# Int8 weights prepared in the first attention, all its projections at the front, and a last stage that interleaves projection and feed-forward

## The chip, the core and the metric

The kernel runs on one core of a Trainium2 chip. The core has a matrix engine (TensorE, in rows PE, its weight loads PEld), three vector-like engines (VectorE or DVE, ScalarE or ACT, GpSimd or POOL) and SyncE (SP), which issues most transfers to sixteen DMA engines. They run their own instruction lists and wait for one another on semaphores. The metric is the device time of one execution in microseconds (us), lower is better.

## The reference, cut to what matters

```
# x: 8 batches x 100 tokens x 512, ctx: 8 x 361 x 128, all float32
x = x + L0_attention(layernorm(x), ctx)      # 16 heads of 32, causal: only 100 context rows count
x = x + L0_experts(layernorm(x))             # 8 experts, 2 per token, hidden 352
x = x + L1_attention(layernorm(x), ctx)      # 16 heads, rotary, latent keys; ends in a product with Wo
x = x + L1_ffn(layernorm(x))                 # I = 1408, both operands quantised

def _quant_dequant(v, axis):
    scale = jnp.maximum(jnp.max(jnp.abs(v), axis=axis, keepdims=True) / 127.0, 1e-8)
    return jnp.clip(jnp.round(v / scale), -127.0, 127.0) * scale

def _L1_ffn_ref(x, w_gate_up, w_down):       # w_gate_up: 2816 x 512, w_down: 512 x 1408
    gate, up = split(quant(x) @ quant(w_gate_up).T)
    h = silu(gate) * up
    return quant(h) @ quant(w_down).T
```

Each weight row (an output) has a scale of its own.

## The kernel before, in words

All engines' lists are written out by hand, stage after stage; float32 products are done as three products of high and low parts (`mm3`, lines 146 to 148).

**First attention.** Normalised tokens are turned and split (`XH`, `XL`); raw weights and context lie in `raw0`, their parts in `hi0` and `lo0` (GpSimd subtracts two of the four pieces). Queries and keys are projected for a pair of batches at a time: 4 groups of 12 + 3 matmuls of 200 columns (`pe_attn0_qk`), the first pair ahead of batch 0, the others within the batch before they are needed; ScalarE evicts queries to `QT`, VectorE keys to `KT`. Per batch: scores with a mask (L1090, L1096), maximum and subtraction on VectorE (L1566, L1572), exponential on ScalarE, turned probabilities (L1112, evicted in L772), product with V (L1127), normalisation on VectorE (L1586, L1591), and one batch later the product with Wout and VectorE's residual add (L1601). The second group of turned probabilities waits for that add, because they share a bank.

**Routing and experts.** Gating, then 20 blocks of 128 token slots. SyncE loads two experts' first weights (1.4 MB each) while the attention runs and six after it, then stores the normalised rows, which GpSimd gathers by index (L603). Folding and the second attention follow.

**Last stage.** `project` (48 matmuls of 512 columns per batch, output in bank 4 or 5) alternates with `pe_weights`: each int8 weight tile (22 of 128 x 512, 4 of 128 x 1408) is loaded by GpSimd, reduced, scaled, rounded by adding and subtracting 1.5 x 2^23, turned on TensorE and evicted to `W1Q` or `W2Q`; the scales are spread to all rows by a product of ones with a diagonal. When all is done the feed-forward runs over the batches (`pe_ffn`): gate/up in four pieces per batch (L1415, 352 columns), SiLU, product on GpSimd, quantisation of h, its transposes (L1424) and the down product (L1432). Gate/up of batch n+1 stands with h and down of batch n.

## Time and profile before

| | us |
|---|---|
| three runs | 948.18, 936.92, 947.85; median 947.85 |
| the profiled execution, its own time | 946.68 |
| its span, first to last instruction | 945.0 |
| TensorE busy in the span | 777.8 (82%), mean granted clock 0.903 |
| VectorE, ScalarE, GpSimd busy | 542.6, 423.3, 250.2 |

Durations are read in the profiled execution, and sums are made against its span. Matmul durations overlap (the engine is pipelined), so the distance of two starts is what a matmul costs in a row of them. "Idle before" names what ended the idle time.

### The profile page before, as it was taken

How to read it: one execution, taken by the hardware profiler on the slowest of the kernel's cores; microseconds unless marked ns; L12 is line 12 of the kernel's file. 1: busy time of each engine (PE TensorE's matmuls, PEld its weight loads, DVE VectorE, ACT ScalarE, POOL GpSimd, SP SyncE). 2: the span in 40 equal slices, each digit the busy share in tenths (PEclk: the TensorE clock that was granted, in tenths of full speed). 3: DMA queues.
4: the chain of work that ended last, by engine and by line, in shares of the span. 5: the costliest groups of instructions: out<-in, count | busy, mean ns of one | idle time of the engine just before them, and what ended most of it. 6: DMA issues, size and time to landing. Idle time of an engine off the chain costs nothing.

```text
span 945.0 us, 14899 instructions
## 1 busy us (share of the span) xinstructions
PE 777.8 (82%) x4828; PEld 621.0 (66%) x4828; DVE 542.6 (57%) x1143; ACT 423.3 (45%) x813; POOL 250.2 (26%) x300
## 2 busy tenths in 40 slices
PE   0789889764999999767889899899878999767774
PEld 0677777664777777767778687787635777554552
DVE  4544346454666664355754745646535767588872
ACT  2432223213555554212763746646634445444441
POOL 1400000012122320440650833616302222123332
PEclk9887889855999999957999999999999999979987
DMA  8400000463565556760010000100164442200000
GB/s 261 169 1 2 0 0 1 170 267 111 158 230 181 171 171 196 250 181 11 12 45 25 30 31 31 43 22 24 36 260 156 141 137 66 75 1 17 18 18 17
DMA packets 28622, 88.25 MB, mean 93 GB/s; under 512 B 6004, under 2 KB 9276, under 8 KB 26272
## 3 DMA queue, kind: packets, MB, share of 16 engines
q1 hardware_dynamic: 23104, 70.49, 21.5%
q0 software_dynamic: 5472, 17.18, 6.6%
q8 instruction: 26, 0.43, 0.2%
q14 instruction: 20, 0.16, 0.1%
HBM read 72.57 MB, written 15.07 MB: 93 GB/s over the span
## 4 chain that ended last, share of the span: by engine, by line
PE 46%; issue 23%; DVE 12%; POOL 8%; DMA 5%; ACT 5%; ACTq 1%; SPq 0%; POOLq 0%; DVEq 0%
PE PS L146 9%; PE PS L148 8%; PE PS L147 8%; POOL wraw L651 5%; PE PS L1061 3%; PE PS L1127 3%; PE PS L1432 2%; PE PS L1415 2%; DMA raw<-wkv_in 1%; ACT w_hi L743 1%; DMA fq_raw<-foldq_in 1%; PE PS L1112 1%; PE PS L1170 1%; DVE xn L126 1%; DMA fp_raw<-foldp_in 1%
## 5 line engine op out<-in xcount | busy, mean ns | idle before, releaser
L651 POOL TENSOR_TENSOR wraw<-wraw,rinv 128x361 f32<-128x361 f32 (+1 forms) x104 | 80.8, 787 | 139.3 <-DVE rinv L1626 139.3
L1466 DVE TENSOR_TENSOR w_lo<-w,w_hi 128x1408 fp32r<-128x1408 f32 x40 | 64.9, 1622 | 36.3 <-ACT w_hi L743 36.3
L834 ACT ACTIVATE wraw<-PS,nmx 128x361 f32<-128x361 f32 (+1 forms) x104 | 58.7, 565 | 38.2 <-DVE nmx L1633 30.4
L1633 DVE TENSOR_REDUCE nmx<-PS 128x1 f32<-128x361 f32 (+1 forms) x104 | 55.0, 530 | 33.7 <-PE PS L148 33.7
L603 POOL DMA_INDIRECT xb<-xn_scratch,rows x20 | 35.9, 1794 | 104.7 <-PE PS L1035 101.6
L743 ACT CAST w_hi<-w 128x1408 fp32r x40 | 54.7, 1370 | 19.4 <-DVE rows L1559 9.7
L146 PE MATMUL PS<-w_hi,xt_hi 128*128 128x352 f32 x160 | 56.9, 356 | 4.9 <-DVE xt_lo L1460 4.6
L1636 DVE TENSOR_TENSOR pt_lo<-PS,pt_hi 128x384 fp32r<-128x384 f32 x96 | 52.3, 547 | 11.9 <-ACT pt_hi L840 11.1
L1226 PE MATMUL PS<-ident,wraw 128*128 128x128 f32 x312 | 52.1, 277 | 6.3 <-POOL wraw L651 3.7
L1061 PE MATMUL PS<-w,ht 128*128 128x512 f32 (+1 forms) x120 | 55.0, 593 | 0.7 <-DVE ht L1478 0.7
L146 PE MATMUL PS<-pf_hi,cx_hi 128*100 128x512 f32 x128 | 51.5, 402 | 3.9 <-DVE pf_lo L1775 3.9
L148 PE MATMUL PS<-w_hi,xt_lo 128*128 128x352 f32 x160 | 52.6, 329 | 0.0
L147 PE MATMUL PS<-w_lo,xt_hi 128*128 128x352 f32 x160 | 52.6, 329 | 0.0
L1226 PEld LDWEIGHTS PS<-ident,wraw 128*128 128x128 f32 x312 | 37.5, 140 | 20.8 <-POOL wraw L651 10.2
L147 PE MATMUL PS<-pf_lo,cx_hi 128*100 128x512 f32 x128 | 51.1, 399 | 0.0
L148 PE MATMUL PS<-pf_hi,cx_lo 128*100 128x512 f32 x128 | 50.8, 397 | 0.0
L840 ACT CAST pt_hi<-PS 128x384 fp32r<-128x384 f32 x96 | 45.5, 477 | 6.2 <-PE PS L1226 6.2
L1415 PE MATMUL PS<-w1q,xqt 128*100 128x352 bf16 x256 | 47.2, 345 | 0.7 <-ACT xqt L985 0.7
L146 PE MATMUL PS<-kt_hi,q_hi 128*128 128x362 f32 (+1 forms) x104 | 42.6, 410 | 3.3 <-ACT wraw L834 1.7
L714 POOL TENSOR_TENSOR h<-sl,us 100x352 f32<-100x352 f32 x32 | 30.0, 937 | 50.2 <-ACT sl L991 35.4
L146 PEld LDWEIGHTS PS<-w_hi,xt_hi 128*128 128x128 f32 x160 | 31.1, 194 | 18.3 <-DVE xt_lo L1460 18.3
L112 PE MATMUL PS<-ident,xn 100*128 100x100 f32 x64 | 11.5, 326 | 36.5 <-DVE xn L126 35.7
(262 smaller groups left out, 2186.7 us busy)
## 6 DMA issues: line engine op xcount, KB each, us to landing
w<-w_in SPq DMA_DIRECT2D x20, 768.0 KB, 5.3
w<-w_in SPq DMA_DIRECT2D x8, 1408.0 KB, 10.6
fq_raw<-foldq_in SPq DMA_DIRECT2D x6, 1088.0 KB, 7.7
cx_raw<-ctx_scratch SPq DMA_DIRECT2D x8, 800.0 KB, 4.9
ctx_scratch<-ctxo SPq DMA_DIRECT2D x24, 256.0 KB, 2.0
wraw<-wup_in POOLq DMA_DIRECT2D x22, 256.0 KB
ys_scratch<-yb SPq DMA_DIRECT2D x20, 256.0 KB
wraw<-wdown_in POOLq DMA_DIRECT2D x4, 704.0 KB
```

Of the source, the lines that this page charges most:

```text
L146: pe.matmul(o, lh, rh, start=start, stop=False)
L147: pe.matmul(o, lh, rl, start=False, stop=False)
L148: return pe.matmul(o, ll, rh, start=False, stop=stop)
L651: pool.tensor_tensor(P1[slot][0:rows, 0:NK], P1[slot][0:rows, 0:NK], rinv[0:rows, jj, t:t + 1].broadcast_to((rows, NK)), ALU.mult).then_in ...
L743: act.copy(WH[which][:, :], w12_of(act_whi.e, which)).then_inc(WHS[which], 1)
L834: act.activation(P1[t % 8][r, 0:NK], PS[r, t % 4, 0:NK], ACT.Exp, bias=nmx[r, jj, t:t + 1], accum_out=rsum[r, jj, t:t + 1]).then_inc(C["ex ...
L1061: last = pe.matmul(PS[:, 4 + i % 2, :], HT[i % 2][0:rows, c * 128:(c + 1) * 128], W3R[i % 2][0:rows, c * D:(c + 1) * D], start=(c == 0), s ...
L1226: last = pe.transpose(PS[:, 4 + t % 3, c * 128:(c + 1) * 128], P1[t % 8][:, c * 128:(c + 1) * 128], ident[:, :])
L1415: last = pe.matmul(PS[0:T, 2 * which + c % 2, 0:GW_], XQT[j][:, k, :], W1Q[:, k, at:at + GW_], start=(k == 0), stop=(k == KC - 1))
L1466: dve.tensor_tensor(WL[which][:, :], w12_of(dve_wlo.e, which), WH[which][:, :].bitcast(F32), ALU.subtract) \
L1633: dve.tensor_reduce(nmx[r, jj, t:t + 1], PS[r, t % 4, 0:NK], AX.X, ALU.max, negate=True).then_inc(C["max"], 1)
L1636: dve.tensor_tensor(pt_place(PTL, t, jj), turned(t), pt_place(PTH, t, jj).bitcast(F32), ALU.subtract) \
```

## The change

1. **Weights in the first attention.** A set is three tiles (even sets: three of gate/up; odd: two and one of down; nine sets, the last with two). Each set is loaded twice: plain (rows on partitions) for the scales, and already turned from a second copy of the weights in memory. VectorE reduces the plain tiles and makes scale and inverse (`dve_scale`). TensorE turns the scales to rows (`turn_scales`), ScalarE copies them out, SyncE stores them and loads the inverses back to all partitions (`share_scales`). GpSimd multiplies the turned set with them, ScalarE adds the constant (`act_magnify`), GpSimd subtracts it to bf16, SyncE stores the result. Ahead of the last stage W1Q, W2Q and the scale rows are loaded whole.
2. **Projections at the front.** All 16 groups (8 of keys, 8 of queries, 400 columns) stand ahead of batch 0, the last four behind batch 0's scores; ScalarE and VectorE evict in turn over four banks, later two. `KT` and part of `QT` lie over `raw0`, so the evictions wait for VectorE's subtraction of the query weights' low part (it was GpSimd's) and GpSimd's of the output weights'.
3. **Transfers.** All eight experts' weights are loaded after the attention, and two fold weights behind the normalised rows.
4. **Last stage.** Projections 0 and 1 run alone, 2 with batch 0's gate/up, and n+3 in four pieces within iteration n of `pe_ffn`, in one bank. Layer norm is done per batch, so ScalarE takes a root (`act_std`) between SiLUs. Rounded tokens and SiLU are written in place.

On VectorE a batch of the first attention in the middle, before, from its normalisation to its statistics:

```order
L1586 RECIPROCAL rs<-PS 100x8 [waits a_pv_xtl]
L1591 TENSOR_TENSOR O<-PS,rs 100x4x32 [waits a_ot,a_rs]
L1591 TENSOR_TENSOR O<-PS,rs 100x4x32
L1586 RECIPROCAL rs<-PS 100x8 [waits a_pv_xtl]
L1591 TENSOR_TENSOR O<-PS,rs 100x4x32 [waits a_rs]
L1591 TENSOR_TENSOR O<-PS,rs 100x4x32
L1601 TENSOR_TENSOR X<-X,PS 100x512 [waits a_op]
L70 BN_STATS stats<-X 100x6 [waits a_res]
```

The same in the new kernel; three reductions, the scale and its inverse come ahead of the residual add:

```order
L1630 RECIPROCAL rs<-PS 100x8 [waits a_pv_xtl]
L1635 TENSOR_TENSOR O<-PS,rs 100x4x32 [waits a_ot,a_rs]
L1635 TENSOR_TENSOR O<-PS,rs 100x4x32
L1630 RECIPROCAL rs<-PS 100x8 [waits a_pv_xtl]
L1635 TENSOR_TENSOR O<-PS,rs 100x4x32 [waits a_rs]
L1635 TENSOR_TENSOR O<-PS,rs 100x4x32
L1713 TENSOR_REDUCE wscale_102<-wraw 128x1 [waits f_dn,w_ldn]
L1713 TENSOR_REDUCE wscale_102<-wraw 128x1 x2
L1716 TENSOR_SCALAR wscale_102<-wscale_102 128x3 [waits w_max]
L1718 RECIPROCAL wscale_102<-wscale_102 128x3 [waits w_sc]
L1645 TENSOR_TENSOR X<-X,PS 100x512 [waits a_op]
L71 BN_STATS stats<-X 100x6 [waits a_res]
```

What moved: the add and the statistics stand five instructions later, behind a wait for loads (`w_ldn`).

On TensorE the end of the feed-forward before; L1415 is gate/up, L1424 the transposes of h, L1432 down:

```order
L1415 MATMUL PS<-w1q,xqt 100x352 x24
L1424 MATMUL PS<-identb,hq 128x100 x11
L1415 MATMUL PS<-w1q,xqt 100x352 x8
L1432 MATMUL PS<-w2q,hqt 100x512 x11
```

A fused iteration from the transposes of h on (L1466; L1457 gate/up, L1446 the next tokens, L1474 down); twelve projection matmuls have come between, of which the first three are shown, then the end:

```order
L1466 MATMUL PS<-identb,wraw 128x100 x11
L147 MATMUL PS<-pf_hi,cx_hi 100x512
L148 MATMUL PS<-pf_lo,cx_hi 100x512
L149 MATMUL PS<-pf_hi,cx_lo 100x512
...
L149 MATMUL PS<-pf_hi,cx_lo 100x512
L1457 MATMUL PS<-w1q,xqt 100x352 x8
L1446 MATMUL PS<-identb,xq 128x100 x4
L1474 MATMUL PS<-w2q,hqt 100x512 x11
```

What moved: the projection of batch n+3, which stood in a stage of its own, now lies between gate/up pieces and around the transposes.

On SyncE, from the last weight loads of the attention to the experts, before:

```order
L454 DMA wraw<-foldq_in 128x2176 x2
L458 DMA w_52<-w_in 128x2816 x2
L461 DMA w_52<-w_in 128x2816 x6
L465 DMA xn_scratch<-XN 100x512 x8
```

and now; the experts' eight stand behind the last scale rows, two weight stores come among the normalised rows:

```order
L513 DMA w_scratch<-wraw 512x1x384
L486 DMA raw_even<-wupt_in 128x4x256
L496 DMA sc_scratch<-scale_rows 2x128 x2
L503 DMA wraw<-sc_scratch 128x256
L530 DMA w_52<-w_in 128x2816 x8
L513 DMA w_scratch<-wraw 512x1x256
L515 DMA w_scratch<-wraw 1408x1x128
L535 DMA xn_scratch<-XN 100x512 x8
L513 DMA w_scratch<-wraw 512x1x256
L539 DMA wraw<-foldq_in 128x2176 x2
```

What moved: two expert loads and the two fold loads, from before the attention to behind it.

```diff
+            def load_plain(n):
+                wait(sp, W["max"], TILES[n])
+                for i, (kind, at) in enumerate(WSETS[n]):
+                    src = wup_d if kind == "up" else wdown_d
+                    sp.dma_start(raw_tile(n, i), src[at * 128:(at + 1) * 128, :]).then_inc(W["ldn"], 16)
+            def load_turned(n):
+                wait(sp, W["sub"], n - 1)
...
+            def share_scales(n):
...
+                sp.wait_ge(ROWSS, n + 1)
...
+                sp.wait_ge(W["scst"], 16 * SHARED[n + 1])
+                wait(sp, W["mul"], TURNED[n - 1] if n >= 2 else 0)
...
+            for n in range(1, B):
+                load_plain(n + 1)
+                share_scales(n)
+                store_set(n - 1)
+                load_turned(n + 1)
+            share_scales(B)
+            sp.wait_ge(A["res"], B)
+            for e in range(NE):
                 sp.dma_start(W12R[:, e, :], w12_d[e]).then_inc(E["w12"], 16)
...
+            for n in range(B + 1):
+                pool.wait_ge(W[f"lt{n % 2}"], 16 * ARRIVED[n + 2])
+                at = 0
+                for buf in parts(n, RAWT[n % 2]):
+                    c, w = buf.shape[1], buf.shape[2]
+                    pool.tensor_tensor(buf, buf, INVB[n % 2][:, None, at:at + w].broadcast_to((128, c, w)), ALU.mult).then_inc(W["mul"], 1)
+                    at += w
+                pool.wait_ge(W["mag"], n + 1)
+                wait(pool, W["st"], 16 * TURNED[n])
+                pool.tensor_scalar(whole(n, STAGE), whole(n, RAWT[n % 2]), MAGIC, None, ALU.subtract).then_inc(W["sub"], 1)
...
+            def batch(n, j):
+                act_scale_rows(n)
                 act_attn0_pt(act, n)
                 if not (isinstance(n, int) and n == 0):
                     act_attn0_oh(act, n - 1)
...
+                if n < B - 1:
                     act_attn0_exp(act, n + 1, 1 - j)
+                if n > 0:
+                    act_magnify(n - 1)
...
+            def turn_scales(n):
+                pe.wait_ge(W["inv"], n + 1)
+                pe.transpose(PS[0:9, 6, 264:392], WSC[n % 2][:, :, :].rearrange("p q t -> p (q t)"), ident[:, :]).then_inc(TURNS, 1)
...
+            def dve_scale(n):
+                par, k = n % 2, len(WSETS[n])
+                dve.wait_ge(W["ldn"], 16 * TILES[n + 1])
+                wait(dve, TURNS, n - 1)
+                for i in range(k):
+                    dve.tensor_reduce(WSC[par][:, 0, i:i + 1], raw_tile(n, i), AX.X, ALU.max, apply_absolute_value=True) \
+                        .then_inc(W["max"], 1)
+                dve.wait_ge(W["max"], TILES[n] + k)
+                dve.tensor_scalar(WSC[par][:, 1, 0:k], WSC[par][:, 0, 0:k], 1.0 / QMAX, QEPS, ALU.mult, ALU.max).then_inc(W["sc"], 1)
+                dve.wait_ge(W["sc"], n + 1)
+                dve.reciprocal(WSC[par][:, 2, 0:k], WSC[par][:, 1, 0:k]).then_inc(W["inv"], 1)
...
+        def pe_attn0_project(pe, g):
+            half, m = g // MT0 % 2, g % MT0
+            mine = slice(m * 128, (m + 1) * 128)
+            if g >= 4:
+                before = g - 4 if g < 14 else g - 2
+                wait(pe, A["qsb" if before % 2 == 0 else "ksb"], before // 2 + 1)
...
+            sp.wait_ge(C["pv"], NG * B)
+            sp.dma_start(W1Q[:, :, :], w1_scratch).then_inc(FFNW, 16)
+            sp.dma_start(S1B[:, :], sc_scratch[0:1, 0:2 * FI].broadcast_to((T, 2 * FI))).then_inc(FFNW, 16)
+            sp.dma_start(W2Q[:, :, :], w2_scratch).then_inc(FFNW, 16)
...
+            def act_std(n):
+                act.wait_ge(LN["var"], n + 4)
+                act.activation(std[:, n:n + 1], veps[:, n:n + 1], ACT.Sqrt).then_inc(LN["std"], 1)
...
+                if n + 4 < B:
+                    low_ctx(n + 4, j)
+                if m:
+                    dve_gate_up(n + 1, 1 - j, 3)
+                if n + 3 < B:
+                    add_out(n + 3)
...
+            def project(n, j, heads):
+                if heads[0] == 0:
+                    wait(pe, O["cxl"], n + 1)
+                    wait(pe, O["res"], n)
+                for h in heads:
...
+            def pe_ffn(n, j):
+                more = n + 3 < B
                 for c in range(GC - 1):
+                    if n + 1 < B:
+                        pe_gate_up(n + 1, 1 - j, c)
+                    if more:
+                        project(n + 3, 1 - j, HEADS[c])
                 pe_ht(n, j)
                 if more:
+                    project(n + 3, 1 - j, HEADS[GC - 1])
```

## Rows read from the trace of the kernel before

**Rows 1.** Table of stretches, us from the span's start; the first row names the columns.

```profile
core 0: us, PE busy (x) PEld busy (x) DVE busy (x) ACT busy (x) POOL busy (x), PEclk, DMA share, GB/s
0.00:48.00 48.00, 20.71 (x117) 16.48 (x118) 25.11 (x39) 18.00 (x27) 14.13 (x11) 0.93 0.64 212
48.00:178.00 130.00, 114.25 (x980) 95.20 (x978) 60.83 (x148) 40.47 (x87) 0.00 (x0) 0.87 0.00 1
...
715.00:822.00 107.00, 103.58 (x556) 75.65 (x556) 68.52 (x143) 48.52 (x56) 24.05 (x47) 0.98 0.38 124
822.00:945.00 123.00, 79.56 (x476) 54.97 (x476) 86.47 (x185) 49.76 (x77) 40.69 (x42) 0.82 0.05 14
```

**Rows 2.** Timeline of TensorE in the last stage: start us, us, instruction, count, idle before.

```profile
715.51 0.47 PE L146 MATMUL PS<-pf_hi,cx_hi 128*100 128x512 f32 x1 [3.95 <-DVE pf_lo L1775]
...
734.76 0.39 PE L147 MATMUL PS<-pf_lo,cx_hi 128*100 128x512 f32 x1
734.99 0.39 PE L148 MATMUL PS<-pf_hi,cx_lo 128*100 128x512 f32 x1
...
849.37 2.64 PE L1432 MATMUL PS<-w2q,hqt 128*100 128x512 bf16 x11
851.85 3.74 PE L1415 MATMUL PS<-w1q,xqt 128*100 128x352 bf16 x24
...
899.78 3.03 PE L1432 MATMUL PS<-w2q,hqt 128*100 128x512 bf16 x11
```

**Rows 3.** Groups of VectorE, 712 to 830: shapes, count, busy us, mean ns, idle before.

```profile
L1799 DVE TENSOR_REDUCE wscale<-wraw 128x1 f32<-128x512 f32 x22 | 15.0, 682 | 0.0
L1771 DVE TENSOR_TENSOR cx_lo<-cx_raw,cx_hi 128x1600 fp32r<-128x1600 f32 x8 | 14.6, 1823 | 9.4 <-ACT cx_hi L943 9.4
...
L1799 DVE TENSOR_REDUCE wscale<-wraw 128x1 f32<-128x1408 f32 x4 | 6.4, 1606 | 0.0
...
L1801 DVE TENSOR_SCALAR wscale<-wscale 128x1 f32<-128x1 f32 x26 | 4.0, 154 | 0.9
```

**Rows 4.** Groups of ScalarE, 702 to 945.

```profile
L943 ACT CAST cx_hi<-cx_raw 128x1600 fp32r<-128x1600 f32 x8 | 12.3, 1542 | 0.0
...
L956 ACT ACTIVATE wraw<-wraw,mgc,wscale 128x1408 f32<-128x1408 f32 x4 | 6.3, 1566 | 6.6 <-DVE wscale L1803 6.6
...
L991 ACT ACT_TABLE_LOAD x1 | 1.3, 1283 | 0.0
```

**Rows 5.** DMA rate in 40 slices of 1.25 us, stretch 176 to 226.

```profile
GB/s 0 0 144 342 415 388 433 433 433 424 433 433 424 433 433 433 424 410 333 209 257 256 252 252 228 28 0 0 0 0 0 0 236 354 252 326 338 159 13 0
```

**Rows 6.** Timeline of TensorE, the first query projection.

```profile
40.16 0.25 PE L146 MATMUL PS<-xnT_hi,hi 128*128 128x200 f32 x1
```

**Rows 7.** Timeline of ScalarE, first eviction of turned probabilities in batches 0, 6, 7.

```profile
56.12 0.49 ACT L772 COPY PT<-PS 100x400 f32<-100x400 f32 x1 [2.02 <-PE PS L1112]
...
153.89 0.49 ACT L772 COPY PT<-PS 100x400 f32<-100x400 f32 x1 [1.46 <-PE PS L1112]
...
164.14 0.49 ACT L772 COPY PT<-PS 100x400 f32<-100x400 f32 x1 [1.47 <-PE PS L1112]
```

**Rows 8.** Timeline of VectorE in batch 6: end of its normalisation, residual add of batch 5.

```profile
162.89 0.49 DVE L1591 TENSOR_TENSOR O<-PS,rs 100x128 f32<-100x128 f32 x2
163.80 0.69 DVE L1601 TENSOR_TENSOR X<-X,PS 100x512 f32<-100x512 f32 x1 [0.42 <-PE PS L148]
```

**Rows 9.** Timeline of the start, VectorE and the GpSimd memset beside it.

```profile
14.53 3.62 POOL L576 MEMSET V<- 100x4224 f32 x1
...
16.75 1.42 DVE L77 TENSOR_SCALAR veps<-mv 100x8 f32<-100x8 f32 x1
```

**Rows 10.** Groups of GpSimd, whole span, each shape apart.

```profile
L581 POOL TENSOR_TENSOR lo<-raw,hi 128x2048 fp32r<-128x2048 f32 x2 | 9.3, 4674 | 6.0 <-ACT hi L866 6.0
...
L574 POOL CAST identb<-ident 128x128 bf16<-128x128 f32 x1 | 0.3, 291 | 13.5 <-DMA mask_f<-mask_in 13.5
```

**Rows 11.** Chain of waits, the first gather of the experts' rows.

```profile
215.44 7.49 DMA xb<-xn_scratch,rows
```

More of the change, by code:

```diff
@@ L53 @@
 NG = -(-RT // 4)
+UPS = D
 LAG = 5
@@ L296, in build_kernel @@
         PFL = sd("pf_lo", [128, NH0, D], F32R)
-        CXR = [sd(f"cx_raw{i}", [128, ROWS]) for i in range(2)]
         CXH = [sd(f"cx_hi{i}", [128, ROWS], F32R) for i in range(2)]
@@ L465, in _ @@
                 sp.dma_start(xn_scratch[b * T:(b + 1) * T], XN[:, b, :]).then_inc(E["xnst"], 16)
+            store_set(B)
+            sp.wait_ge(W["st"], 16 * TURNED[B + 1])
+            for i in range(2):
+                sp.dma_start(FQR[i], foldq_d[i]).then_inc(C["fq0"], 16)
             def load_block(i):
@@ L1115, in pe_attn0_pv @@
         def pe_attn0_pv(pe, n, j):
-            if j == 0 and not (isinstance(n, int) and n == B - 2):
-                wait(pe, A["qsb"], 2 * n + 2 * MT0)
-                wait(pe, A["ksb"], 2 * n + 2 * MT0)
+            if isinstance(n, int) and n == 0:
+                pe.wait_ge(A["qsb"], 8)
+                pe.wait_ge(A["ksb"], 8)
             for g in range(2):
@@ L1278, in batch @@
                     pe_attn0_out(pe, n - 1)
-            batch(0, 0, 1)
-            pe.wait_ge(A["wlo2"], 2)
-            with pe.Fori(0, B // 2 - 2) as p:
-                batch(2 * p + 1, 1)
-                batch(2 * p + 2, 0, p + 2)
-            for n in range(B - 3, B):
+                turn_scales(n + 1)
+            for n in range(B):
+                if n == 1:
+                    pe.wait_ge(A["wlo2"], 1)
                 batch(n, n % 2)
@@ L1375, in _ @@
+            HEADS = [range(h, h + 4) for h in range(0, NH0, 4)]
             pe.wait_ge(O["pfl"], NH0)
-            def pe_weights(n, odd, p=None):
-                for i, (kind, _) in enumerate(wtiles(n if p is None else (p,), odd)):
-                    wait(pe, W["sub"], 3 * n + i + 1)
-                    wait(pe, W["ev"], 3 * (n - 1) + i + 1)
-                    ch = KC if kind == "up" else IC
-                    for c in range(ch):
-                        last = pe.transpose(wbank(i, ch)[:, c, :], WQT[i][:, c * 128:(c + 1) * 128], identb[:, :])
-                    last.then_inc(W["tr"], 1)
-                    wait(pe, W["dg"], 3 * n + i + 1)
-                    wait(pe, W["sb"], 3 * (n - 2) + 3)
-                    pe.matmul(PS[0:T, 6 + odd, i * 128:(i + 1) * 128], ones[:, :], diag[i][:, :], start=True, stop=True) \
-                        .then_inc(W["bc"], 1)
@@ L1389, in _ @@
[L1389 to L1395 removed]
             def pe_xq(m, j):
                 wait(pe, F["sub"], m + 1)
[L1400 to L1401 removed]
                 wait(pe, F["xev"], m)
+                wait(pe, F["hev"], 2 * (m - 1))
@@ L1683, in batch @@
                     dve_attn0_shift(dve, n + 1, 1 - j)
-                if queries is not None:
-                    dve_attn0_k(dve, queries)
                 dve_attn0_norm(dve, n)
+                dve_scale(n + 1)
                 if not first:
                     dve_attn0_add(dve, n - 1)
-            batch(0, 0, 1)
-            with dve.Fori(0, B // 2 - 2) as p:
-                batch(2 * p + 1, 1)
-                batch(2 * p + 2, 0, p + 2)
-            for n in range(B - 3, B):
+            for n in range(B):
                 batch(n, n % 2)
@@ L1917, in _ @@
                     dve_hmax(0, 0, c - 1)
-            with dve.Fori(0, B // 2 - 1) as p:
-                dve_ffn(2 * p, 0)
-                dve_ffn(2 * p + 1, 1)
-            dve_ffn(B - 2, 0, False)
-            dve_hmax(B - 1, 1, GC - 1)
-            dve_hscale(B - 1, 1)
-            dve_hsub(B - 1, 1)
-            dve_out(B - 1, 1)
+            dve_xq(1, 1)
+            dve_xsub(1, 1)
+            add_out(2)
+            low_ctx(3, 1)
+            for n in range(B):
+                dve_ffn(n, n % 2)
 def rope_tables():
```

520 lines of the change are left out of this document (241 added, 279 removed).

## The prediction

> **What bounds the kernel now.** I read the table of stretches first [rows 1], then the timelines inside the three stretches that the change touches. The program is a chain of stages. The first attention fills about 40 to 178, routing and the start of the experts 178 to 223, experts and second attention 223 to 690 (untouched), the output projection with the weight preparation about 715 to 822, the int8 feed-forward 822 to 945. TensorE is busy 97% of the projection stretch, at a granted clock of 0.98, and only 65% of the feed-forward, at 0.82: there VectorE is the longer (86 of 123). GpSimd does nothing in the first attention. So the idle TensorE of the feed-forward is what a fused last stage can fill, and the idle GpSimd and the empty DMA queues of the first attention are what the weight preparation can use.
>
> **The last stage, fused.** A projection matmul of 512 columns starts every 0.23 us (two rows in succession, [rows 2]), so one batch has 48 x 0.23 = 11.1 us, and the eight have 88.6. The stage from 715.5 to 822 is 106: the rest is the int8 weights on TensorE (132 transposes, 26 scale matmuls) and the last set's wait. In the feed-forward one batch has 32 matmuls of 352 columns, 24 of them in 3.74 at the full clock, so about 4.7, eleven of 512 columns in 2.6 [rows 2], and 15 small transposes, about 1: 8.3 us, where VectorE makes the period about 12.9.
> Fused, a batch of TensorE work is 11.1 + 8.3 = 19.4, and some 0.3 for the twelve switches between banks: 19.7. VectorE has 86.5/8 = 10.8 per batch there [rows 1], plus the low part of the context 1.8 [rows 3], plus the residual add and statistics 0.7 each with two small ones: 14.5. ScalarE has 49.8/8 = 6.2, plus a cast of 1.5, plus two table loads of 1.3 [rows 4] that the root between SiLUs now costs: 10.3. Both hide under 19.7, so TensorE is the bound and its clock stays near 1.
> In order of time: projections 0 and 1 alone, 715.5 + 22.2 = 737.7. Then transposes and the eviction of the first tokens, 1; gate/up of batch 0 with projection 2, 4.7 + 11.1, and 2 for the context low part, which stands behind the first evictions on ScalarE and VectorE; then 3 for the activations of batch 1, which VectorE takes up only after batch 0's last gate/up: 759.5. Five fused iterations (n = 0 to 4) are 98.5, with 2 more for the late context of projection 3: 860.0. After the fifth down matmul the work is that of before: there it ended at 902.8 [rows 2] and the span at 945.0, so 42.2: 902.2. **The last stage gives 43**. Ends: 48 if those waits vanish, 30 if each fused iteration takes 22 (the handshakes with VectorE now sit between four pieces of a projection).
> The finished weights must be back by 738: W1, W2 and two broadcast rows are 5.65 MB, issued at about 706 behind the folding loads. At 433 GB/s [rows 5] that is 13 us, at the 212 GB/s of the start [rows 1] 27: 719 to 733. Hidden by projections 0 and 1, narrowly at the slow end.
>
> **The first attention: projections at the front.** Before: 240 matmuls of 200 columns in four portions, 0.11 apart, each eviction waited for. The first projection starts at 40.2 [rows 6] and batch 0's probabilities are evicted at 56.1; the three portions inside the batches go. The two unrolled batches without a portion stand 10.25 apart [rows 7]. After: 120 matmuls of 400 columns, by the 512-column row about 0.18 each: 21.6, with evictions on two engines in turn over two or four banks. The first subtraction on GpSimd becomes VectorE's (2048 columns, about 2.4) and its block on VectorE's normalisations goes, so keys start about 38. With scores for two batches (3) batch 0 turns at about 63.5, against 56; batch 1 ten later, at 73.5. If nothing else were added, seven batches of 10.3 and the tail would end near 150, 28 before 178.1.
>
> **What the weights put back.** Per batch VectorE gets three reductions (0.68 each, or one of 1.61), a scalar op of 0.15 [rows 3] and a reciprocal about as short: 2.4 for even sets, 3.3 for odd, 2.9 in the mean. They stand between the normalisation of a batch, which ends at 163.4, and the residual add at 163.8 [rows 8]: only 0.4 of idle. Behind them wait the add, the next batch's second transpose group (it waits for that add) and the transpose of the scale rows, for which TensorE waits before it turns the next probabilities. So nearly all of it is in the path: 10.3 + 2.9 - 0.4 = 12.8.
> The scalar op also meets GpSimd. The row at 16.75 took 1.42 for eight columns, and ended when the memset beside it did; such an op elsewhere takes 0.15 [rows 3, 9]. In the new order GpSimd subtracts set n-1 (1536 or 2432 columns) just when ScalarE has magnified it (about 1.7 or 2.7 by [rows 4]) after the exponentials, which is when VectorE comes to that scalar op. The subtraction has one input: by the memset 0.86 ns a column, by the two-input subtraction 2.28 [rows 9, 10], so 1.3 to 5.5 us. I take the cheap end, since the one-input cast row (0.29 for 128, start included) lies below the two-input rate. Then the scalar op waits 0.4 to 1.1: +0.8. Dear end: +3.
> The Trainium skill (GPSIMD Engine Reference, Engine selection) says one-input work there is "roughly line-rate" and two-input work about twice as slow as VectorE. That agrees with the side that I took; by a two-input rate on both the batch would be 2 longer.
> The ring over two batches: the subtraction of set n-1 must end before SyncE stores it, loads set n+1 turned and set n+2 plain, and VectorE reduces that. Traffic is 8.65 MB twice, 4.3 MB of bf16 out: 2.4 MB per set, 5.5 us at 433 GB/s, 11 at 212, and seven issues of 0.4 with some 2 to land. Two batches then need about 1.5 (turn) + 7 (to the exponentials' end) + 2 + 1.8 + 3 + 8 + 2 + 2.9 = 28, or 14 a batch: just above 13.6. Odd sets have more small pieces (512 bytes in, 256 out), so I take 14.3. The granted clock of 0.87 may fall with TensorE idle a third of the time; that is in the range.
> The Trainium skill (DMA: Bandwidth & Descriptors, Specifications) asks for transfers of at least 512 bytes, and says that below it the engine does read-modify-write. By that rule the 256-byte stores of the turned down weights cost more than their 0.36 MB, and rival A gains; no row of before has stores so narrow.
> Batch 7 then turns at 73.5 + 6 x 14.3 = 159.3, and the tail of 14 (164.1 to 178.1, [rows 7]) ends at 173.5. **The attention gives 4.5.** Ends: 12.6 a batch gives 15; 17 a batch costs 12.
>
> **Routing.** All eight experts' weights now load after the attention, 11.5 MB instead of 8.65: 27 us instead of 20, the row stores and one weight store behind them, so 212 to 215 on the old clock, against the routed rows at 215.4 [rows 11]. Nearly hidden. The fold weights (2.2 MB) move from the start to just here and share the queues with the first gather, and GpSimd's last two sets block some normalisations, which are scalar ops. **+2.5**; ends 0 and +7. The first gather, its own 7.5 [rows 11], is what comes late if the stores slip.
>
> **Sum.** -4.5 + 2.5 - 43 = -45. The profiled execution: span 945.0, time 946.7. So 900 and 1.7: **902**. The median of before, 947.85, is 1.2 above that execution; one of its three runs was 936.9.
>
> **Rivals.**
> A. The weight ring sets the attention: GpSimd at its dear rate or narrow stores and loads at half rate. The ring is then 34 to 40 for two batches, 17 to 20 each, +16 to +34 over seven: 918 to 936. For: every set is in series through four engines and one queue. Against: the empty queues (1 GB/s). Chance 0.17.
> B. The ring has slack, GpSimd's port costs nothing, the period is 12.6 or less: 886 to 892. 0.13.
> C. The fused stage stays a chain of handshakes: the add that frees the projection's only bank, or the root on ScalarE before the next SiLU, comes late by 3 to 4 in each of five iterations. +15 to +20: 917 to 922. Against: VectorE has 5 idle per iteration. 0.06.
> D. Slower than before: rival A's mechanism at its worst, loads of both forms and stores one behind another with each landing waited for. It decides from 14.3 + (45 + 19)/7 = 23.4 us per batch, above 967. It needs 2.4 MB to take over 20 us. 0.03.
> E. It does not do what it says: the feed-forward waits for the stored weights (a broadcast row is read 100 times). At 124 GB/s, the mean of the old stretch [rows 1], they land at 751: +13, 915. 0.04.
> The forecast itself, 892 to 914, has 0.57.
>
> **Numbers.** 884 to 924 leaves out the upper part of A, D and a little of B. A change within 2% is about what a measurement of this kernel can tell from none; faster by over 2% is under 928.9. Of A a third lies above that, D is slower: faster 0.91, same 0.06, slower 0.03.
>
> **What would show it.** The residual add of batch 7 at about 173; attention batches 13 to 15 apart, with VectorE's scale reductions ending just before TensorE goes on; a scalar op of 1 us or more beside a GpSimd op; the routed rows some 37 after that add; the down matmuls of batches 0 to 4 some 19.7 apart with TensorE's clock near 1, then 12 to 13. Wrong would be: scale reductions that wait for a DMA (A), down matmuls over 22 apart (C), TensorE idle on DMA before its first gate/up (E).

## The result, and the profile after

| | before | after |
|---|---|---|
| median of 20 runs each, us | 947.54 | 936.39 |
| lowest and highest | 936.8 to 951.7 | 929.5 to 941.0 |
| the profiled execution's span | 945.0 | 938.7 |
| VectorE, GpSimd busy | 542.6, 250.2 | 548.3, 301.9 |

The ratio is 0.9888 (95% interval 0.9867 to 0.9909): 1.1% faster, where 4.8% was forecast. The last stage gave what was forecast and the first attention took most of it back. Of all executions one, 902.22 us in run 9, was in the chip's slower state, and it is counted in no ratio and no median below. The table of stretches, to be read against [rows 1]:

```profile
core 0: us, PE busy (x) PEld busy (x) DVE busy (x) ACT busy (x) POOL busy (x), PEclk, DMA share, GB/s
48.00:205.00 157.00, 124.76 (x883) 100.80 (x881) 102.10 (x183) 52.71 (x92) 70.46 (x19) 0.71 0.41 126
205.00:250.00 45.00, 24.08 (x160) 23.25 (x160) 28.07 (x87) 10.59 (x16) 14.68 (x9) 0.55 0.87 339
...
751.00:765.00 14.00, 13.13 (x50) 8.98 (x51) 2.70 (x3) 0.00 (x0) 0.00 (x0) 0.88 0.86 264
...
777.00:801.00 24.00, 19.24 (x86) 13.48 (x86) 12.70 (x24) 6.22 (x10) 3.78 (x4) 0.86 0.10 35
...
824.00:899.00 75.00, 75.00 (x422) 54.41 (x420) 56.26 (x112) 38.89 (x52) 20.13 (x20) 1.00 0.08 27
```

I cut the program at two events that both traces have, here and in every run below: the start of the last residual add of the attention ("last add") and the first gather. Before: 177.4 and 215.4. After: 204.95 and 250.2. So the attention costs 27.6, the routing 45.2 instead of 38.0, and from the gather to the end it is 688.5 instead of 729.6, 41.1 less: the three make the -6.3 of the span.

**The attention.** ScalarE's first evictions of turned probabilities in batches 0, 1, 5, 6 and 7 (compare [rows 7]):

```profile
66.36 0.89 ACT L827 COPY PT<-PS 100x400 f32<-100x400 f32 x2 [1.80 <-PE PS L1162]
...
76.61 0.49 ACT L827 COPY PT<-PS 100x400 f32<-100x400 f32 x1 [0.41 <-PE PS L1162]
...
149.54 0.49 ACT L827 COPY PT<-PS 100x400 f32<-100x400 f32 x1 [0.41 <-PE PS L1162]
...
166.68 0.49 ACT L827 COPY PT<-PS 100x400 f32<-100x400 f32 x1 [0.41 <-PE PS L1162]
...
186.83 0.49 ACT L827 COPY PT<-PS 100x400 f32<-100x400 f32 x1 [0.41 <-PE PS L1162]
```

From batch 3 on the batches are 17.1 and 20.15 apart in turn (18.4 in the mean from batch 1 to 7), not 14.3. VectorE's timeline in batch 4 shows one place where time is lost, and GpSimd's stands under it:

```profile
140.12 2.80 DVE L1713 TENSOR_REDUCE wscale<-wraw 128x1 f32<-128x512 f32 x3
142.96 5.23 DVE L1716 TENSOR_SCALAR wscale<-wscale 128x3 f32<-128x3 f32 x1
148.22 0.18 DVE L1718 RECIPROCAL wscale<-wscale 128x3 f32<-128x3 f32 x1
148.31 0.65 DVE L1645 TENSOR_TENSOR X<-X,PS 100x512 f32<-100x512 f32 x1
```

```profile
141.81 6.35 POOL L674 TENSOR_SCALAR wraw<-raw_odd 128x2432 bf16<-128x2432 f32 x1 [8.36 <-ACT raw_odd L932]
148.13 3.44 POOL L670 TENSOR_TENSOR raw_even<-raw_even,wraw 128x1536 f32<-128x1536 f32 x1
```

Three columns take 5.23 us and end when GpSimd's subtraction does (148.16). Two things are to be seen besides: the last and longest of the reductions (to 142.92) ran beside that subtraction at its usual rate, as all three did in batch 1 (1.87 us), and the reciprocal and the residual add ran beside the multiplication. In batches 1 to 6 this operation took 2.0, 5.2, 3.1, 5.2, 3.0, 5.2; with GpSimd idle it takes 0.17. And the subtraction itself takes 6.35 for 2432 columns, 2.6 ns each, where I had taken 0.86.

The chain of waits over the two batches that follow (start, us, what):

```profile
139.41 2.32 ACT raw_odd L932
...
141.81 6.36 POOL wraw L674
148.19 0.57 SPq L513
...
149.49 0.83 SPq L486
...
151.56 1.33 SPq L480
...
153.41 6.97 DMA wraw<-wup_in
160.41 1.88 DVE wscale L1713 x3
162.31 3.02 DVE wscale L1716
...
176.71 2.32 ACT raw_odd L932
```

This is a second loop: magnify, subtract, store and turned loads issued, plain tiles issued and landed at 160.4, reduced, then 11.2 us to the next magnifying of an odd set (scale rows, TensorE's transposes and scores, maximum, exponentials), 37.3 us for two batches. From one trace it can't be told which of the two loops binds: the wait for GpSimd lies in both, and the tiles land just as VectorE comes to them (no reduction waits for a DMA). Run 2 decides it below.

A third thing lengthens both: TensorE's clock. It was 0.87 in this stage before and is 0.71 now. At the end of batch 2 TensorE stands idle for 6.3 us until the blocked operation and the reciprocal are through. Then mask and scores take nearly twice what they take in run 5 (second piece), where only one set is worked on:

```profile
111.16 0.38 PE L1324 MATMUL PS<-ident,wscale 128*9 128x128 f32 x1 [6.31 <-DVE wscale L1718]
...
114.22 1.54 PE L1141 MATMUL PS<-maskb,identb 100*100 100x400 bf16 x4
115.69 1.67 PE L1146 MATMUL PS<-raw,QT 32*100 32x100 f32 x32
```

```profile
125.64 0.84 PE L1142 MATMUL PS<-maskb,identb 100*100 100x400 bf16 x4
126.41 0.96 PE L1147 MATMUL PS<-raw,QT 32*100 32x100 f32 x32
```

The granted clock is 0.50 over 111 to 117 here, the lower level of 1.2 GHz, and 0.97 over 80 to 150 in run 5. From the first transpose (111.34) to the first maximum (117.38) it is 6.0 us at the lower clock, all in the path, so about 3 of the 18.4 may be the clock's. That is an estimate: no run changes the clock and nothing else.

**The routing.** VectorE behind the last add, and GpSimd beside it:

```profile
209.42 0.20 DVE L80 RECIPROCAL rstd<-std 100x8 f32<-100x8 f32 x1 [2.17 <-ACT std L85]
209.66 4.02 DVE L1759 TENSOR_TENSOR wg_lo<-wg_raw,wg_hi 128x32 fp32r<-128x32 f32 x1
213.60 3.45 DVE L1762 TENSOR_SCALAR XN<-X,mv,rstd 100x512 f32<-100x512 f32 x2
```

```profile
207.95 6.35 POOL L674 TENSOR_SCALAR wraw<-raw_odd 128x2432 bf16<-128x2432 f32 x1 [2.44 <-ACT raw_odd L932]
214.27 2.50 POOL L670 TENSOR_TENSOR raw_even<-raw_even,wraw 128x1024 f32<-128x1024 f32 x1
```

Before, these two took 0.19 and 1.00, and the root came 0.27 after its input. Now magnifying set 7 stands ahead of the root (+1.9), and 3.8 and 2.45 are waits for GpSimd: 8.2, about the 7.2 lost. In run 4, where GpSimd doesn't subtract set 7, both are back at 0.19 and 1.00.

**The last stage.** The down matmuls of batches 0, 1, 4 and 5 (compare [rows 2]):

```profile
820.72 2.54 PE L1474 MATMUL PS<-w2q,hqt 128*100 128x512 bf16 x11
839.65 2.54 PE L1474 MATMUL PS<-w2q,hqt 128*100 128x512 bf16 x11
...
896.39 2.54 PE L1474 MATMUL PS<-w2q,hqt 128*100 128x512 bf16 x11
909.11 2.60 PE L1474 MATMUL PS<-w2q,hqt 128*100 128x512 bf16 x11
```

The fused iterations are 18.9 apart, TensorE is busy all of 824 to 899 at a granted clock of 1.00, and no gate/up waits for a DMA.

### The profile page after: what moved, and what is told of

Its sections match the earlier page's. It is cut to its first block, busy times and chain, and to the rows that moved or that the text cites. A ratio compares the mean times of both kernels' runs of the same rounds, so it can differ in the third digit from the quotient of the medians.

```text
span 938.7 us, 13466 instructions
## 1 busy us (share of the span) xinstructions
PE 770.4 (82%) x4533; PEld 613.3 (65%) x4533; DVE 548.3 (58%) x1077; ACT 417.8 (45%) x790; POOL 301.9 (32%) x268
## 4 chain that ended last, share of the span: by engine, by line
PE 40%; issue 22%; DVE 12%; POOL 9%; DMA 6%; ACT 6%; SPq 2%; ACTq 1%; POOLq 0%; DVEq 0%
PE PS L147 8%; PE PS L149 8%; PE PS L148 8%; POOL wraw L741 5%; PE PS L1457 3%; PE PS L1118 3%; ACT w_hi L793 2%; PE PS L1474 2%; PE PS L1162 1%; DMA raw<-wkv_in 1%; POOL wraw L674 1%; DMA fq_raw<-foldq_in 1%; DVE wscale L1716 1%; PE PS L1220 1%; DMA fp_raw<-foldp_in 1%
## 5 line engine op out<-in xcount | busy, mean ns | idle before, releaser
L768 POOL TENSOR_TENSOR wraw<-gs,us 100x352 f32<-100x352 f32 x32 | 30.4, 949 | 155.7 <-ACT gs L1038 127.3
L147 PE MATMUL PS<-pf_hi,cx_hi 128*100 128x512 f32 x128 | 55.2, 431 | 8.9 <-DVE pf_lo L1833 3.7
L1680 DVE TENSOR_TENSOR pt_lo<-PS,pt_hi 128x384 fp32r<-128x384 f32 x96 | 52.3, 546 | 12.0 <-ACT pt_hi L895 11.2
L147 PE MATMUL PS<-kt_hi,q_hi 128*128 128x362 f32 (+1 forms) x104 | 42.6, 410 | 3.3 <-ACT wraw L889 1.6
L1457 PE MATMUL PS<-w1q,xqt 128*100 128x352 bf16 x256 | 44.2, 319 | 1.3 <-ACT xqt L1033 1.3
L113 PE MATMUL PS<-ident,xn 100*128 100x100 f32 x64 | 11.8, 333 | 34.3 <-DVE xn L127 33.5
```

Source lines behind the costliest of these rows:

```text
L147: pe.matmul(o, lh, rh, start=start, stop=False)
L1457: last = pe.matmul(PS[0:T, 2 * which + c % 2, 0:GW_], XQT[j][:, k, :], W1Q[:, k, at:at + GW_], start=(k == 0), stop=(k == KC - 1))
L1680: dve.tensor_tensor(pt_place(PTL, t, jj), turned(t), pt_place(PTH, t, jj).bitcast(F32), ALU.subtract) \
```

## The experiments

The time behind the first gather varies from run to run: where no edit touches it, it took 677 to 692 us. So I read events in the stretch that is edited, but they are from one execution each and vary too. With the same attention the last add stands at 204.95, 200.8 and 201.5 (the changed kernel, runs 6 and 12), at 171.5, 162.9 and 166.9 (runs 7, 8, 9) and at 148.7 and 151.5 (runs 5 and 11). From it to the gather, where nothing there was edited (runs 1, 2, 3, 6, 7), it is 44.9 to 48.0. Differences below 4 us, below 9 from run 7 on, say nothing by themselves, and a gain of the whole kernel is read from the ratio, which is against the kernel before.

**1. Take the scalar operation out.**

```diff
-dve.tensor_reduce(WSC[par][:, 0, i:i + 1], ...)
-dve.tensor_scalar(WSC[par][:, 1, 0:k], WSC[par][:, 0, 0:k], 1.0 / QMAX, QEPS, ALU.mult, ALU.max)
+dve.tensor_reduce(WSC[par][:, 1, i:i + 1], ...)
...
-act.activation(t, t, ACT.Identity, bias=mgc[:, 0:1])
+act.activation(t, t, ACT.Identity, bias=mgc[:, 0:1], scale=float(QMAX * QMAX))
-act.copy(SROW[:, :], PS[0:9, 6, 264:392])
+act.activation(SROW[0:6, :], PS[0:6, 6, 264:392], ACT.Copy, scale=1.0 / QMAX)
```

> The three-column scalar operation between the weight-scale reductions and their reciprocal on VectorE (2.0 to 5.2 us in batches 1 to 6 of the changed kernel, 0.17 where GpSimd is idle) is taken out: its factor 1/127 goes into ScalarE's copy of the scale rows and its square into the magnifying pass; the floor of 1e-8 on the weight scales is left out. Port theory (the operation waits for GpSimd's subtraction and that sets the period of 17.1 and 20.2 us): the reciprocal follows the reductions at once, periods 14.1 and 15.1, last residual add of the attention at about 180 instead of 205, about 910 in all. Ring theory (magnify, subtract, store, load, reduce in series over two batches sets it or is next): magnify to landed load is 21 us and landed load to the next magnify 13.3 without the wait, 34.3 per two batches, last add at 196, about 928. If neither holds (the reductions' own time sets it): no change, 936.

Measured: 928.41, ratio 0.9782 (0.9751 to 0.9813); last add at 193.6. That is what was expected if the second loop is next (196 and 928). VectorE now waits where it didn't:

```profile
152.39 1.87 DVE L1713 TENSOR_REDUCE wscale<-wraw 128x1 f32<-128x512 f32 x3 [5.22 <-DMA wraw<-wup_in]
154.30 0.18 DVE L1716 RECIPROCAL wscale<-wscale 128x3 f32<-128x3 f32 x1
```

The four waits of this kind are 3.2, 2.2, 5.2 and 9.5 us. The wait for GpSimd was real, and under it the ring was nearly as long.

**2 and 3. Issue the plain tiles ahead of the store; alone, and with edit 1.**

```diff
+load_plain(2)
 for n in range(1, B):
-    load_plain(n + 1)
     share_scales(n)
+    if n + 2 <= B:
+        load_plain(n + 2)
     store_set(n - 1)
     load_turned(n + 1)
```

> Only SyncE's order changes: the plain tiles of set n+2 are issued before the store of set n-1, not after it. Port theory: the reductions still end inside GpSimd's subtraction, no change, 936 (934 to 938). Ring theory: the plain tiles land 5 to 9 us earlier, period 2 to 4 shorter, 912 to 922.

> Both edits together. Port theory with the ring as the next bound: this reaches what the first edit alone can't, periods of about 14.1 and 15.1, last add at 180, about 910. Port theory with a slack ring: the same as the first edit alone. Reductions theory: 936.

Alone: 938.1, ratio 0.9864 (0.9826 to 0.9902), no change from the changed kernel. The last add is at 201.6, where runs 6 and 12 have it with the loads in the old order, the batches are 18.0 apart as in those two, and the scalar operation still takes 5.2 in all three odd sets. So the ring doesn't bind while the operation waits for GpSimd. With edit 1: 918.02, ratio 0.9663 (0.9633 to 0.9692), last add at 181.3, with 180 expected; the expected time of 910 wasn't reached (the kernel before had 950.4 in these rounds). So two bounds lie over each other: against the changed kernel's 204.95, taking the first away gives 11.4 of the last add, both 23.7, and the second alone nothing that can be told. By the ratios it is 10 us for the first and 21 for both. The first, and with it every run below that contains it, also leaves out the floor of 1e-8 on the weight scales.

**4. Move the subtraction instead.**

```diff
 act.activation(t, t, ACT.Identity, bias=mgc[:, 0:1])        # magnify
+if n < B:
+    act.activation(whole(n, STAGE), t, ACT.Identity, bias=mgn[:, 0:1])   # mgn = -MAGIC
```

> The subtraction of sets 0 to 7 moves from GpSimd (4.1 and 6.35 us) to ScalarE (about 1.6 and 2.3, behind the magnifying pass); the scalar operation on VectorE stays. Port theory: the scalar operation takes 0.17 again unless GpSimd's multiplication (3.4 to 5.5) now meets it, and the ring is 2 to 4 shorter: periods about 15, last add about 182, 912 to 918. If the multiplication meets it instead, nothing is gained. Ring theory: 2.5 to 4 less per set, last add about 192, 922 to 926.

Measured: 917.01, ratio 0.9636 (0.9594 to 0.9678), last add at 186.7, between the two expectations for it (182 and 192), the time in the first's range. The scalar operation is still there, in batch 5 too:

```profile
147.96 1.87 DVE L1721 TENSOR_REDUCE wscale<-wraw 128x1 f32<-128x512 f32 x3 [3.63 <-DMA wraw<-wup_in]
149.87 0.17 DVE L1724 TENSOR_SCALAR wscale<-wscale 128x3 f32<-128x3 f32 x1
```

0.17 to 0.20 in all batches: it was GpSimd's subtraction, and nothing else, that it had waited for.

**5. Only one set of weights.** Sets 1 to 8 are neither loaded nor worked on.

```diff
-for n in range(1, B): load_plain(n + 1); share_scales(n); store_set(n - 1); load_turned(n + 1)
+# set 0's staged tiles and rows are stored in all places, once
-dve_scale(n + 1)            # in VectorE's batch
-turn_scales(n + 1)          # in TensorE's batch
```

> Only set 0 of the int8 weights is made, its staged tiles and scale rows are stored in the places of all the others in one go during the attention, and sets 1 to 8 are neither loaded nor worked on (the feed-forward so runs on wrong weights); the projections at the front, the routing and the fused last stage stay. It separates the gain of the projections at the front from the cost of the weight work in the attention. If moving the projections gains what I forecast (batches 10.3 apart, as the unrolled pair before) batch 7 turns at about 66.4 + 7 x 10.5 = 140 and the last residual add is at about 153; with GpSimd idle in the routing the 7 us there come back too: 876 to 884. If batches without projections are slower than 10.3 for another reason, the last add is past 160 and the time above 890.

Measured: 876.35, ratio 0.9274 (0.9201 to 0.9346); last add at 148.7. TensorE's clock is 0.97 over 80 to 150, where the changed kernel has 0.67 over 75 to 205. VectorE's residual adds are 10.25 apart:

```profile
113.00 0.69 DVE L1645 TENSOR_TENSOR X<-X,PS 100x512 f32<-100x512 f32 x1 [0.42 <-PE PS L149]
123.25 0.69 DVE L1645 TENSOR_TENSOR X<-X,PS 100x512 f32<-100x512 f32 x1 [0.42 <-PE PS L149]
```

By these executions the projections at the front give 28.7 (25.9 by run 11), and the weights put back 56.3. The first gather came 38.0 after the last add, exactly as before the change, though all eight experts' weights load there; it then waited for the row stores.

**6. Undo the fusion alone.**

```diff
-for n in range(2):
-    project(n, n, range(NH0))
+for n in range(B):
+    project(n, n % 2, range(NH0))
...
-more = n + 3 < B
+more = False          # in pe_ffn; split_ctx, act_std, low_ctx, add_out go ahead of it likewise
```

> The changed kernel with the last stage alone undone: all eight projections first, each waiting for the residual add of the one before on its only bank, then the feed-forward of all batches as before the change. My account: eight projections of 11.1 and about 1.2 of add between them are 98, the feed-forward 123 as before, less one batch's transition, so 218 to 221 instead of 188: 966 to 970. If the stage got shorter only because the weight preparation left it (17 to 18 us) and the fusion itself adds nothing, it stays at 936 to 942.

Measured: 968.75, ratio 1.025 (1.020 to 1.030). Its projections stand 12.17 apart (11.1 and the add), its feed-forward fills the last 122 us at a clock of 0.86. The stage takes 220.4 from the first projection to the end, against 187.8 fused and 229.5 before: the fusion is worth about 33 us, the leaving of the weights the other 9 of the 41.

**7. The reductions to the start of the batch.** Edit 1, and:

```diff
 def batch(n, j):                             # VectorE
+    dve_scale(n + 1)
     dve_attn0_max(dve, n + 1, 1 - j)
     ...
-    dve_scale(n + 1)
...
+load_plain(2); share_scales(1); load_plain(3)
+for n in range(2, B + 1):                    # SyncE
+    share_scales(n); load_plain(n + 2); store_set(n - 2); load_turned(n)
```

> The scalar operation taken out as in the first run, the reductions and the reciprocal of set n+1 moved to the start of batch n (VectorE has about 5 us there until TensorE's scores), and SyncE's order changed to: scale rows of set n, plain tiles of n+2, store of n-2, turned tiles of n. Port and ring theory: VectorE's weight work is then hidden, the period falls to 11 to 12 (10.3 of the attention itself; GpSimd 9.7 a batch in the mean), last residual add at 158 to 165, 892 to 900. If a ring over three batches (turned load, multiplication behind the last set's subtraction, magnifying) still sets it: 13 to 14 a batch, last add 172 to 178, 905 to 912.

(TensorE's turn of the scale rows also waits for the normalisation of the batch before.) Measured: 902.0, ratio 0.9533 (0.9482 to 0.9583), last add at 171.5 (162.9 and 166.9 in runs 8 and 9, the same up to there). The time lies between the two expectations. From batch 1 to 7 the periods are 13.7, 11.0, 11.6, 15.9, 10.3 and 16.5, 13.2 in the mean: near the longer ring's 13 to 14. GpSimd in one of the long ones:

```profile
105.53 3.53 POOL L673 TENSOR_TENSOR raw_even<-raw_even,wraw 128x1536 f32<-128x1536 f32 x1
113.12 4.08 POOL L677 TENSOR_SCALAR wraw<-raw_even 128x1536 bf16<-128x1536 f32 x1 [4.07 <-DMA w_scratch<-wraw]
117.25 5.48 POOL L673 TENSOR_TENSOR raw_odd<-raw_odd,inv_odd 128x1024 f32<-128x1024 f32 x2
```

It waits for the store of the set before, which leaves the only staging buffer.

**8, 9 and 12. The routing.** Edit 8 on top of 7; 12 is the same on the changed kernel; 9 has the second piece too.

```diff
-act_magnify(B - 1)                            # ahead of the root
+# magnify and subtract set 7 on ScalarE, behind the high-part copies of tokens 1 and 3
-store_set(B - 1)                              # ahead of the row stores
+# behind the fourth row store
+if n == B: pool.wait_ge(LN["xn"], 2 * B)      # set 8's multiplication
...
+# edit 9: GpSimd's three products for tok_of ahead of set 8's subtraction
```

> The run before, and in the routing: set 7 is magnified and subtracted by ScalarE between its high-part copies of batches 1 to 4, so that neither stands ahead of the root nor holds GpSimd; set 8's multiplication waits until the last token is normalised; set 7 is stored behind the fourth row store. The routing took 44.5 us from the last residual add to the first gather, 37.4 before the change: if the magnifying ahead of the root (2.3) and VectorE's two operations that waited for GpSimd (4.0 and 3.4 us, alone 0.2 and 1.0) are the cause, it comes back to 38 to 39: 5 to 6 less than the run before, 886 to 895. If the 11.5 MB of expert weights and the fold weights delay it, nothing.

> The changed kernel with the routing edits of the eighth run alone (set 7 magnified and subtracted on ScalarE inside the copies, set 8's multiplication after the last normalisation, set 7 stored behind the fourth row store). The logits come 6.5 to 7 earlier after the last add (31.9 us now, 24.9 before the change). If the products behind set 8's subtraction take most of that back as they did there: 2 less than the changed kernel, 933 to 935. If not: 929 to 931.

> The eighth run with GpSimd's three token products ahead of set 8's subtraction instead of behind it (that subtraction waited until 202.3 for set 7's store, and the products stood behind it until 205.2, though VectorE had their input at about 198). If that queue is what took back the gain of the normalisation (45.9 us from the last add to the first gather against 48.0 without the routing edits, where the logits came 6.8 earlier), the first gather comes 3 to 4 earlier, 42 after the last add, bounded then by the subtraction itself: 896 to 899. If the landing of the row stores behind 11.5 MB of weights is the bound, no change from 902.

(The expectation of 8 counts from the end of the add; from its start it is 45.2 after the change and 38.0 before.) Measured: 8 is 902.1 (0.9533, 0.9489 to 0.9576), not the 886 to 895 expected and no better than 7, though its gather comes 45.9 after the last add instead of 48.0. 12 is 933.99 (0.9874, 0.981 to 0.9939), gather after 42.65 instead of 45.2: in its expected range, but its median does not differ from the changed kernel's by more than the intervals. 9 is 894.77 (0.9459, 0.9361 to 0.9558), just below its range, gather after 42.6. (It also puts two memsets behind the products, with TensorE's wait for them.) In 8 VectorE's two operations are short again, the logits stand 28.3 after the add instead of 35.1, and GpSimd gives most of it back:

```profile
202.29 2.77 POOL L684 TENSOR_SCALAR wraw<-raw_even 128x1024 bf16<-128x1024 f32 x1 [16.16 <-DMA w_scratch<-wraw]
...
205.16 0.72 POOL L692 TENSOR_TENSOR tok_of<-in_blk,route 100x320 bf16<-100x320 bf16 x1
```

In the changed kernel the missing 7 us are the root and the two waits for GpSimd. A third bound lay under them: the products queued behind a store that lands only after 11.5 MB of weights. There they didn't wait for it (GpSimd idled 3.5 before them, for VectorE's indices); it came to bind when the first two were gone. Run 9 is still 4.6 above the 38.0 of before, its gather waiting for the row stores; how that splits wasn't tried.

**10. All subtractions on ScalarE, in the gap behind the evictions** (on top of 9).

```diff
 act_attn0_pt(act, n)
+if n > 1: act_subtract(n - 2)
```

> The ninth run with all subtractions of sets 0 to 7 on ScalarE, each in the gap behind the probabilities' evictions of the next batch (ScalarE idles 2 to 3 us there, the pass takes 1.6 or 2.3). GpSimd keeps the multiplications alone and they start as soon as their tiles land. In the seventh run GpSimd's chain of subtraction, multiplication and the store's landing set 5 of 7 periods (mean 12.6, against 10.25 with one set only). If that serial chain is the remaining bound: 10.5 to 11.5 a batch, last add at 150 to 157, 885 to 892. If the transfers are (7 us from issue to landing): 12 or more, no better than 896.

Measured: 891.69 (0.9454, 0.939 to 0.9518), by the ratio the same as 9, and the last add came at 169.6, not at 150 to 157. GpSimd is no longer the bound, it waits for the turned tiles in all of sets 2 to 7. The issue of the turned load of set 3 and the wait for it:

```profile
104.60 5.61 SPq L487 DMA_DIRECT2D raw_odd<-wupt_in  x1
...
116.51 5.53 POOL L678 TENSOR_TENSOR raw_odd<-raw_odd,inv_odd 128x1024 f32<-128x1024 f32 x2 [13.07 <-DMA raw_odd<-wdownt_in]
```

My reading of run 7 as GpSimd's chain fell: with it removed the transfers hold the same place. The trace has two things more. Right behind the store in 256-byte pieces the issue of this load takes 5.61 and, for set 5, 2.90 us (3.93 and 4.34 in run 7), where it is 0.83 in the changed kernel. And TensorE falls to the lower clock in the long batches: 0.50 over 127 to 141, where it is 1.00 over 96 to 108. Whether bytes, small pieces, the order on the one queue or the clock is the limit wasn't tried. Runs 9 and 10 are the best versions: the changed kernel's work in another order and without the scalar operation and the floor, 5.4% below the kernel before where the change alone has 1.1%.

**11. What an operation on GpSimd costs.** Seven operations on the idle engine in the one-set kernel.

> The one-set kernel with seven operations on the idle GpSimd during batches 2 to 6, each waited for: a memset of 1536 columns, scalar subtraction to bf16 and to float32 (1536), copy to bf16 (1536) and in float32 (768), product of two 768-column inputs and of 1536. My prediction had 0.86 ns a column for one input. By the subtraction's rows (4.08 for 1536) the float32 to bf16 form will take 4.1 again; if the conversion is the cost, the float32 form and the copies take 1.3 to 2 for 1536; if any one-input arithmetic costs it, only the copies and the memset are short; if every read of SBUF costs it, only the memset.

```profile
96.06 1.38 POOL L682 MEMSET raw_odd<- 128x1536 f32 x1 [8.03 <-DVE X L1658]
97.53 4.09 POOL L683 TENSOR_SCALAR raw_odd<-raw_odd 128x1536 bf16<-128x1536 f32 x1
101.70 4.09 POOL L684 TENSOR_SCALAR raw_odd<-raw_odd 128x1536 f32<-128x1536 f32 x1
105.85 1.46 POOL L685 CAST raw_odd<-raw_odd 128x1536 bf16<-128x1536 f32 x1
107.38 0.83 POOL L686 COPY raw_odd<-raw_odd 128x768 f32<-128x768 f32 x1
108.29 1.81 POOL L687 TENSOR_TENSOR raw_odd<-raw_odd 128x768 f32<-128x768 f32 x1
110.18 2.75 POOL L688 TENSOR_TENSOR raw_odd<-raw_odd 128x1536 f32<-128x1536 f32 x1
```

This is one execution. Memset, cast and copy take 0.9 to 1.1 ns a column, the scalar subtraction 2.66 to either type, a product of two inputs 1.8 (both the same columns) to 2.4. It is the arithmetic with a constant that costs, not the conversion and not the read.

## Why the prediction was wrong

**The last stage (-43): right in sum, with errors that cancel.** 187.8 from the first projection (750.9) to the end, against 229.5: -41.7. The start was longer: the down matmuls of batch 0 end 72.3 after the first projection, where my sum had 63.7. Projection 0 ran at a clock of 0.88 (13.8 us to the next, 0.9 of it a wait, for 11.1 of work), and gate/up of batch 0 with projection 2 took 23 instead of 17.8, at 0.86. The four further iterations took 75.7, forecast about 81 with the late context, and the tail 39.8 instead of 42.2. Run 6 shows the fusion as a gain of its own. Rival C (handshakes) and rival E (late weights) didn't come.

**The projections at the front (28 alone): right.** Run 5 has 28.7 and a period of 10.25.

**Where the attention's 32 us went.** The last add was forecast at about 172.6 and came at 204.95. Batch 1 turned its probabilities 3.1 late (76.6 for 73.5), the six periods had 18.4 for 14.3 (24.4), and from batch 7's turn to the last add it was 18.1, where the trace of before has 13.3 and the sum took it over without the last set's work (4.8).

**The weights in the attention (+23.5 in my sum, 56.3 measured): this step failed.** It said "I take the cheap end, since the one-input cast row (0.29 for 128, start included) lies below the two-input rate", so 0.86 ns a column and "+0.8" for the scalar operation. The row didn't say that: 0.29 for 128 columns is 2.27 ns each, the two-input rate of 2.28, unless a start that no row gave is taken off. A cast is indeed cheap (0.95 in run 11), but the instruction in the diff is a subtraction of a constant: 2.66. The wait for GpSimd was therefore 1.9 to 5.1 us a batch, 3.8 in the mean, and I had written "Dear end: +3". That the subtraction falls "just when ScalarE has magnified it", "which is when VectorE comes to that scalar op", was right.
The Trainium skill (GPSIMD Engine Reference, Engine selection) has one-input work "roughly line-rate". By run 11 that holds for copies and casts and not for scalar arithmetic, which is dearer than two inputs; it had seemed to agree with the cheap end.

**The ring (28 for two batches, 14.3 taken) was mis-sized too.** The chain above has 37.3. Magnifying and subtraction took 8.8 of it, where the sum has 2 and 1.8; reductions, blocked operation and reciprocal 5.1 for 2.9; the way from there to the next magnifying 11.2 for 1.5 and 7, with TensorE at the lower clock. From the subtraction's end to the landed plain tiles it is 12.2, against 3, 8 and 2: that part was right. The clock had been left to the range, and it isn't in the sum.

**Rival A came true in its numbers and only in part in its mechanism.** Its 17 to 20 a batch holds the 18.4, its 918 to 936 ends at the measured 936.4. But its sign, scale reductions that wait for a DMA, isn't in the trace, and shortening the ring alone changed nothing (run 2). It is the next bound: with the scalar operation gone four reductions do wait (run 1). What spoke for it in the prediction, "every set is in series through four engines and one queue", was right; against it I put only the empty queues, which says nothing of latency. Of the 56.3, run 1 gives back 11.4 without the scalar operation, run 3 23.7, run 7 33.5 with the reductions hidden (38 to 42 in runs 9 and 8, the same attention). What remains, 14 to 23, stands behind transfers and the clock (run 10), and their own limit is open.

The narrow stores were not it in the changed kernel: 352 KB in 256-byte pieces landed in 4.3 us in the median, 384 KB in 768-byte pieces in 3.3. The Trainium skill's rule on transfers below 512 bytes (DMA: Bandwidth & Descriptors, Specifications) points the right way, and here it is worth 1 us a set at most. In runs 7 and 10 the slow issues behind these stores may be more of it; that wasn't tried.

**Routing (+2.5, ends 0 and +7): 7.2.** I had the mechanism in half a sentence, "GpSimd's last two sets block some normalisations", and priced it at nearly nothing. The transfers that I did price were hidden (run 5). The root on ScalarE behind a 2.3 us magnifying pass wasn't in the sum.

**The chances.** Rival A had 0.17. The forecast's range of 892 to 914 rested on GpSimd's cheap rate and on a short ring, and both fell on the dear side. That the time lies at rival A's upper end is luck in part: what set the period was the forecast's own path at its dear end.

## What to carry to other kernels

A rate for an engine has to come from a row of the same instruction kind: copy, scalar arithmetic and two-input arithmetic are three prices on GpSimd. A three-column operation in a serial chain can cost what GpSimd's instruction beside it costs, so put into such chains only operations that ran beside GpSimd undisturbed here (reductions, reciprocals, an add with one operand in PSUM), or fold their factor into a pass that exists. When work is put beside a loop, write down its own loop from buffer to buffer with every issue and landing and compare the periods: the average DMA load (0.41 here) says nothing of it, and each bound removed here uncovered another close below.

## What was unexpected of the hardware

- A wait costs TensorE more than the wait. After 6.3 us of idling the clock was 0.50 and mask and scores took 1.54 and 1.67 us instead of 0.84 and 0.96; over the attention it was 0.71, before the change 0.87.
- GpSimd's subtraction of a constant is slower (4.09 us for 1536 columns) than its product of two inputs (2.75 to 3.45).
- VectorE's reductions, its reciprocal and its add with a PSUM operand ran at full speed beside GpSimd, where the scalar operation of 3 columns (5.23 instead of 0.17) and a 32-column subtraction with both inputs in SBUF (4.02 instead of 0.19) stood until GpSimd's instruction ended, the second by its row until 0.6 us before that end. The Trainium skill (SBUF — State Buffer, Who interferes with whom) says so: such operations and GpSimd exclude one another for a whole instruction, and reductions never contend. The traces agree with 5.23 and 4.02 us on the one side and reductions at their usual 0.68 on the other.
